# Two-layer graph attention on one core: new timetables for the first two and last three pairs, and another buffer for two output tiles

## The reference, cut to what matters

```
h = maximum(layernorm(x), 0)                      # layer 0
q, k, v = h @ Wq + bq, h @ Wk + bk, h @ Wv + bv   # 8 heads of 64
weights = softmax(q @ k.T / 8 + mask)             # mask: -1e9 where adj == 0
x = x + weights @ v
h = maximum(layernorm(x), 0)                      # layer 1
q, k, v = h @ Wq.T, h @ Wk.T, h @ Wv.T
rel = adj.T * (q @ k.T)
rel = rel / norm(rel, axis=2)
x = x + rel @ v
```

## Time and profile before

| | |
|---|---|
| device time, median of 3 runs | 2420.07 us (2419.92 to 2421.03) |
| profiled execution | 2422.38 us, span 2420.6 us |
| PE busy | 2391.3 us, 99% of the span |
| ACT busy | 1686.1 us, 70% |
| DVE busy | 1454.1 us, 60% |
| POOL busy | 1301.7 us, 54% |

### The profile page before, as it was taken

How to read it: one execution, slowest core, us unless ns; L and a number is a source line. 1 busy time by engine, 2 the same in 40 slices (tenths; PEclk the granted TensorE clock), 3 DMA queues, 4 the chain that set the end, 5 groups by cost and what they waited for, 6 DMA issues and landing times.

```text
span 2420.6 us, 53556 instructions
## 1 busy us (share of the span) xinstructions
PE 2391.3 (99%) x19252; PEld 1299.4 (54%) x19252; DVE 1454.1 (60%) x4435; ACT 1686.1 (70%) x4111; POOL 1301.7 (54%) x1159
## 2 busy tenths in 40 slices
PE   8999999999999999999999999999999999999998
PEld 4455555555555555555555555555555555555554
DVE  5665666655666555665556665556655566655664
ACT  5867777667776677776777766777667777667773
POOL 3655555555555555555555555555555555555561
PEclk9999999999999999999999999999999999999999
DMA  7756676666677566776566765667755667656663
GB/s 206 148 123 125 136 152 140 135 129 130 133 153 140 115 131 133 153 141 128 128 131 144 149 137 121 132 132 153 143 127 127 132 146 149 131 124 135 134 125 70
DMA packets 938361, 328.09 MB, mean 136 GB/s; under 512 B 886000, under 2 KB 886256, under 8 KB 938096
## 3 DMA queue, kind: packets, MB, share of 16 engines
q1 hardware_dynamic: 935312, 319.43, 63.3%
q10 hardware_dynamic: 2784, 5.24, 0.6%
HBM read 72.88 MB, written 33.55 MB: 44 GB/s over the span
## 4 chain that ended last, share of the span: by engine, by line
PE 90%; DMA 2%; ACT 2%; DVE 2%; issue 1%; POOL 1%; DVEq 0%; SPq 0%; ACTq 0%
PE B L728 76%; PE S L804 7%; PE O L728 7%; DMA probs_t<-halves 2%; ACT probs L529 1%; DVE stats L592 0%; ACT h L473 0%; ACT halves L537 0%; DVE masked L665 0%; POOL v L423 0%; DVE rel_halves L699 0%; POOL halves L427 0%; ACT h_halves L480 0%; DVE result L706 0%; DVE v_sum L657 0%
## 5 line engine op out<-in xcount | busy, mean ns | idle before, releaser
L427 POOL TENSOR_TENSOR halves<-probs,halves 128x512 f16<-128x512 f32 x512 | 598.1, 1168 | 561.5 <-ACT halves L537 561.2
L529 ACT ACTIVATE probs<-masked,neg_max 128x256 f32<-128x256 f32 x1024 | 508.3, 498 | 204.4 <-DVE neg_max L665 204.2
L665 DVE CUSTOM_DVE_ANT_0 masked<-S,mask 128x256 f32<-128x256 f32 x1024 | 385.7, 415 | 129.8 <-PE S L804 125.5
L413 POOL TENSOR_TENSOR h_halves<-h,h_halves 128x512 f16<-128x512 f32 x256 | 295.3, 1159 | 155.7 <-ACT h_halves L480 155.7
L728 PE MATMUL B<-wv,h0t 128*128 128x512 f16 x1536 | 354.1, 380 | 3.9 <-DMA h0t<-h_halves 2.5
L728 PE MATMUL B<-h0t,wq 128*128 128x512 f16 x1536 | 352.8, 379 | 0.0
L728 PE MATMUL B<-h0t,wk 128*128 128x512 f16 x1536 | 352.5, 379 | 0.0
L728 PE MATMUL B<-h1t,wm 128*128 128x512 f16 x1488 | 336.5, 379 | 1.3 <-DMA h1t<-h_halves 1.3
L728 PE MATMUL B<-wvt,h1t 128*128 128x512 f16 x1488 | 336.7, 379 | 1.1 <-issue 1.1
L537 ACT ACTIVATE halves<-probs 128x512 f16<-128x512 f32 x512 | 322.6, 630 | 20.3 <-PE O L728 4.2
L728 PEld LDWEIGHTS O<-v,probs_t 128*128 128x128 f16 x6144 | 245.8, 98 | 126.1 <-DMA probs_t<-halves 9.9
(11 more groups left out here) (78 smaller groups left out, 2983.0 us busy)
## 6 DMA issues: line engine op xcount, KB each, us to landing
x_in<-in_x_dram SPq DMA_DIRECT2D x128, 256.0 KB, 3.1
out_dram<-result SPq DMA_DIRECT2D x128, 256.0 KB, 3.4
x_res<-in_x_dram SPq DMA_DIRECT2D x124, 256.0 KB, 3.3
probs_t<-halves SPq DMA_TRANSPOSE x512, 2.8
h0t<-h_halves SPq DMA_TRANSPOSE x132, 3.2
h1t<-h_halves SPq DMA_TRANSPOSE x124, 3.3
rq<-in_L_gnn_Wq_dram ACTq DMA_DIRECT2D x4, 256.0 KB, 4.9
x_res<-in_L_gnn_Wk_dram ACTq DMA_DIRECT2D x4, 256.0 KB, 5.4
```

The costliest lines, as they stand in the source:

```text
L413: nc.gpsimd.tensor_tensor(h_halves[:, n, 1, :], h[:, n % 2, :], h_halves[:, n, 0, :], ALU.subtract).then_inc(h_low[layer], 1)
L427: nc.gpsimd.tensor_tensor(halves[:, n % RING, 1, :], probs[:, n % 2, :, :].rearrange("p t n -> p (t n)"), halves[:, n % RING, 0, :], ALU.s ...
L529: ins = nc.scalar.activation(probs[:, n % 2, i, :], masked[:, n % 2, i, :], ACT.Exp, bias=neg_max[:, n % 2, i:i + 1], scale=-1.0, accum_ou ...
L665: ins = nc.vector.tensor_tensor_reduce(out=masked[:, n % 2, i, :], in0=S[n % 4][:, i, :], in1=mask[:, i, :], scale=SCORE, scalar=BIG, op0= ...
```

## The change

It gives new slots to the steps of pairs 0 and 1 and of pairs 29, 30 and 31, and it writes the third and fourth output tile of pair 31 into `h` (the buffer of the normalized matrices, which has two tiles as `result` has) with a wait on the last low half of `h` in the place of the wait on the stores.

```diff
-    PRODUCT_0 = {("v", 0): 0.5, ("v", 1): 1, ("q", 0): 1.5, ("k", 0): 2.5, ("v", 2): 5, ("v", 3): 7,
-                 ("q", 1): 9, ("k", 1): 10, ("q", 2): 13, ("k", 2): 13.5, ("q", 3): 15, ("k", 3): 22.5}
+    PRODUCT_0 = {("v", 0): 0, ("v", 1): 1, ("q", 0): 2, ("k", 0): 4, ("q", 1): 5.5, ("v", 2): 7.5,
+                 ("k", 1): 8, ("v", 3): 9, ("q", 2): 13.5, ("k", 2): 15.5, ("q", 3): 16.5, ("k", 3): 22.5}
...
+        def out_buffer(n, p):
+
+            return (h if p == PAIRS - 1 and n >= 2 else result)[:, n % 2, :]
+
...
-                    sp.dma_start(ov[p][:, n, :], result[:, n % 2, :]).then_inc(stored[n % 2], 16)
+                    sp.dma_start(ov[p][:, n, :], out_buffer(n, p)).then_inc(stored[n % 2], 16)
...
-                    need(dve, stored[n % 2], 16 * (2 * p + n // 2))
-                    nc.vector.scalar_tensor_tensor(result[:, n % 2, :], B[BANK[kind, n, p]][:, :], 1.0 / WS,
+                    if p == PAIRS - 1 and n >= 2:
+                        dve.wait_ge(h_low[1], TILES * PAIRS)
+                    else:
+                        need(dve, stored[n % 2], 16 * (2 * p + n // 2))
+                    nc.vector.scalar_tensor_tensor(out_buffer(n, p), B[BANK[kind, n, p]][:, :], 1.0 / WS,
```

More of the change, by code:

```diff
@@ L90, in adjacency_attention_two_layers @@
-    PRODUCT_30 = {("rq", 0): 41, ("rq", 1): 42, ("rq", 2): 43, ("rq", 3): 44, ("rel", 0): 45.5,
-                  ("rel", 1): 46, ("rv", 0): 47, ("rv", 1): 48.5, ("rv", 2): 49, ("out", 0): 49.5,
-                  ("rv", 3): 50, ("out", 1): 50.5, ("out", 2): 51, ("out", 3): 51.5}
-    LAYER1_30 = {"ln1_scale": [36.5], "ln1_apply": [37, 37, 38, 38], "ln1_split": [37.5, 37.5, 38, 39],
-                 "squares": [45.5, 46], "rel_scale": [47, 47.5], "rel_split": [47.5, 49]}
-    PRODUCT_31 = {("q", 0): 0.5, ("k", 0): 1, ("v", 0): 2.5, ("q", 1): 4, ("v", 1): 4.5, ("k", 1): 6,
[3 rows of a table removed]
-                  ("out", 0): 41, ("out", 1): 42, ("out", 2): 44, ("out", 3): 46}
@@ new lines, in adjacency_attention_two_layers @@
+    SCORED_0 = [6.5, 11, 19, 26]
+    MASKED_0 = [6.5, 8.5, 12, 13.5, 19, 23.5, 25, 27]
+    MULTIPLIED_0 = [12.5, 12.5, 14, 14, 18.5, 21, 21, 21, 25.5, 27, 28, 28.5, 31, 31.5, 32.5, 34]
+    LAYER0_0 = {"x_res": [10.5, 10.5, 12, 12.5], "residual": [16, 20, 29, 32]}
+    LAYER0_1 = {"x_in": [-27.5, -25, -19.5, -17], "ln0_stats": [-14, -14, -13, -12.5], "ln0_power": [-12.5],
+                "ln0_scale": [-11], "ln0_apply": [-9, -9, -6, -2], "ln0_split": [-7, -7, -5, -2]}
+    PRODUCT_1 = {("v", 0): -2, ("v", 1): 1.5, ("q", 0): 2.5, ("k", 0): 3, ("v", 2): 4.5, ("v", 3): 8.5,
+                 ("q", 1): 9.5, ("k", 1): 10, ("q", 2): 13, ("q", 3): 13.5, ("k", 2): 15, ("k", 3): 23}
@@ new lines, in adjacency_attention_two_layers @@
+    OUT_29 = {("out", 0): 64, ("out", 1): 65, ("out", 2): 66, ("out", 3): 66.5}
+    PRODUCT_30 = {("rq", 0): 41, ("rq", 1): 42, ("rq", 2): 43.5, ("rq", 3): 44, ("rel", 0): 45.5,
+                  ("rel", 1): 46, ("rv", 0): 47.5, ("rv", 1): 48.5, ("rv", 2): 49, ("out", 0): 49,
+                  ("rv", 3): 50, ("out", 1): 50.5, ("out", 2): 51, ("out", 3): 51.5}
+    LAYER1_30 = {"ln1_scale": [36.5], "ln1_apply": [37, 37.5, 38, 38], "ln1_split": [38] * TILES, "squares":
+                 [45.5, 47.5], "rel_scale": [47, 48], "rel_split": [48, 49.5]}
@@ new lines, in adjacency_attention_two_layers @@
+    PRODUCT_31 = {("q", 0): 0, ("v", 0): 0.5, ("k", 0): 1.5, ("q", 1): 3.5, ("v", 1): 5, ("k", 1): 5.5,
[3 rows of a table added]
+                  ("out", 0): 41.5, ("out", 1): 44, ("out", 2): 44.5, ("out", 3): 49.5}
+    SCORED_31 = [3.5, 7.5, 12.5, 15]
+    MASKED_31 = [3.5, 5.5, 8, 9.5, 12.5, 13.5, 15, 16]
+    MULTIPLIED_31 = [7.5, 8, 9.5, 9.5, 12, 12, 12, 12.5, 15, 15, 15, 16.5, 18, 18, 18.5, 19.5]
+    RESIDUAL_31 = {"residual": [10, 14.5, 17.5, 17.5]}
+    LAYER1_31 = {"ln1_stats": [21.5, 21.5, 22.5, 22.5], "ln1_power": [23], "ln1_scale": [23.5], "ln1_apply":
+                 [24, 24.5, 24.5, 25], "ln1_split": [24, 24.5, 25, 25], "squares": [37, 37.5], "rel_scale":
+                 [38.5, 39], "rel_split": [38.5, 40.5]}
```

## The result

| | before | changed |
|---|---|---|
| device time, median of 7 runs each | 2420.74 us (2419.92 to 2421.72) | 2411.16 us (2409.97 to 2413.34) |
| ratio | | 0.9961, 95% interval 0.9952 to 0.997 |
| profiled span | 2420.6 us | 2408.4 us |

A forecast was written before the change was run, and what follows sets the result against it. PE, busy 99% of the span, was taken as the bound, with gaps winnable only at the two ends. Start −5.6 and end −4.3 sum to −9.9 us, from median 2420.07 to 2410.2 us; range 2405.5 to 2416.5.

The forecast's parts named there:

- The start, −5.6: From the second scores to the first `rv`: PE's gaps shrink by 5.6 us in sum, new waits included.
- −3.5 at `v0.1`: First `h0t` of pair 1: its wait falls from 2.52 to 0.45 us and full clock returns 1.44 us.
- The end, −4.3: From `h1t` of pair 30 to the last store: PE saves 4.3 us in sum, new waits included.
- The clock's 1.33 returned: At `out2.30`: with only 0.9 us of wait left, the product runs at full clock and saves 1.33 us.
- +0.5 at `rq0.31`: At `rq0.31`: a new wait of 0.5 us, since PE is now faster than the fourth tile of `h`.
- `out3.29`, +0.1: At `out3.29`: PE waits 0.1 us more.
- 1.26 of `h1t`: Pair 30: `h1t` lands before PE asks for it, so its wait of 1.26 us goes.
- one of my signs of being wrong: Anywhere walked as free: a wait of over 1 us there would show the prediction wrong.
- the port rival: Layer-norm scales of pairs 1, 30, 31: each meets one more blocking POOL operation, +3.0 us, 2413.2 us; chance 0.12.
- The side engines set the start: Start: the chain to `h0t` moves only with ACT's fifth `exp`, gaining 2.8 us, total 2413.0 us; chance 0.15.
- The change does nothing: Start's gaps only move, as later pairs keep the old tables: 2420 us, give or take 2; chance 0.1.
- slower through the store of `out0.29`: Pair 29: a later-issued store holds DVE at `out2.29`, and PE waits; 12.5 us late gives 2421 us; chance 0.06.

The follow-up runs named there:

- e1: The new tables of pairs 0 and 1 alone, put into the kernel before: 2415.57 us, ratio 0.9981.
- e4: The kernel before with only the loads of `x_res` of pair 0 issued earlier: 2420.61 us, ratio 1.0.
- e11: The kernel before with only `residual0.31` moved early, from slot 15 to 10: 2423.16 us, one run.
- e8: The kernel before with only the new slots of the products and scores of pair 0: 2418.53 us, ratio 0.9997.
- e2: The new tables of pairs 29, 30 and 31 alone in the kernel before, without the other output buffer: 2418.30 us, ratio 0.9992.
- e3: The kernel before with only the third and fourth output tile of pair 31 written into `h`: 2420.51 us, ratio 1.0.
- e9: The changed kernel with only `residual0.31` moved late, from slot 10 to 13: 2412.14 us, ratio 0.9963 against the kernel before.
- e5: The kernel before with the new residual and layer-norm order of pair 31 and a few late steps of pairs 30 and 31: 2417.76 us, ratio 0.9992.

## Why the prediction was right, and where not

**The start, −5.6: right in sum.** Measured −6.07 in the profile, −4.6 by e1's ratio. The 6.07 is all in PE's gaps: from the first `v0.0` to the first `rv` they are 7.38 us before, with 1.44 more for the slow product, and 2.75 us after. The waits at the second scores, at `k1.1` and at the first `rv` went as walked; `k1.1` even lost the 0.95 that I had left it. New waits came at other sizes: `h0t` 1.01 (I said 0.45), `q0.1` 0.42 (1.0), and two for `probs_t` that I had not walked to, 0.58 and 0.74 us. I had written that no `pv` is asked for within 3 us of its transpose; that is wrong, and the 0.53 that I took off for it is not a gain. `q0.1` came 4.61 us nearer to the first `v0.0`, 0.35 of it because one `pv` now stands behind it; my terms up to it add to 4.45. The 73.9 that I named for its start is not what these terms give (79.49 − 4.45 = 75.04, or 74.69 with the `pv`), and it stood at 75.43.

**The reason given for the largest term was wrong.** Of the −3.5 at `v0.1`, 1.44 us was "the clock's, returned". e4 (full clock, `q0.1` at 55.76) and e11 (full clock, 55.81, behind waits of 0.54 and 0.91 us for `probs_t`) show that the low clock cost nothing here; PE would have waited for ACT instead. The gain came since ACT's `exp` and halves moved with PE: the fourth high half of `h` stands 3.39 us earlier in the changed kernel, where I had written 4.05. e8 shows it from the other side: with the products alone ACT moves 0.97 us and the first `rv` 0.8 us.

**The end, −4.3: too large; measured −2.65 in the profile, −2 by e2's ratio without the buffer.** Two terms failed.

- *"The clock's 1.33 returned" at `out2.30`.* I added it beside the wait, and put +0.5 at `rq0.31` for PE now being faster than the fourth tile. e3 shows that this tile was late by 1.42 us already as soon as the clock doesn't fall. What counts is how much earlier the tile itself comes: PE waits for it at 29.37 us behind `rel0.30` in e3 and at 26.11 in the changed kernel. PE's own −0.8, −2.04 and −1.33 are not all to be had beside it: I had −3.7 from `rel0.30` to `rq0.31`, and 29.25 to 26.11 is −3.14.
- *`out3.29`, +0.1 where the wait grew by 0.87.* That ate most of the 1.26 of `h1t`, which did go. e9 and e11 show the cause: a second POOL operation beside the scale of pair 30, where my walk had counted one. From `rv0.29` to `rel0.30` I had −0.36; with that operation out of the way e9 has −0.33, in the changed kernel it is +0.75. (A wait of 0.34 us for `k_st` at a `scores` some 55 us ahead of `rel0.30` was in neither walk nor rival; e9 has it too.) A wait of over 1 us at a place walked as nearly free was one of my signs of being wrong, and here it stood. This was the port rival, to which I gave 0.12. It asked for one more such meeting in each of pairs 1, 30 and 31; it came in pair 30 alone (in pair 31 all these operations take 0.16 us, in pair 1 two take 1.56 together where one took 1.13), and cost 1.08 us and not 3. The Trainium skill, "SBUF — State Buffer", section "SBUF: two separate sides", has DVE held for the whole of POOL's operation where both want the shared port pair and POOL's began first; by that rule the trace agrees, 1.08 us beside a POOL operation of 1.15, and where nothing stands beside it 0.16.

The other terms: `pv10.31` +0.9, measured 0.61 + 0.20 there; 0.45 at `rel0.30` stays, measured 0.45; `rv1` −0.8, its wait is gone; 0.9 left at `out2.30`, measured 0.87; last store −0.2, measured −0.24 in e3. The walk's "31 periods" between 166 and 2240 us are 28, at 74.1 us each (2149.22 for 29); no term hangs on it.

**The sum** was −9.9 from 2420.07, and the median fell by 9.6 (7.3 to 11.6 by the ratio's interval). By the markers the parts I had walked gave 8.7 and not 9.9: the start 0.5 us more than I had, the end 1.65 less. So the agreement of −9.9 with −9.6 is in part chance: errors of both signs, and the scatter of the medians. The 0.9 us between 8.7 and 9.6 is within what the medians leave open.

**The other rivals.** "The side engines set the start" was right on who sets it (e4) and wrong on the sum, since the change moves them too. "The change does nothing" and "slower through the store of `out0.29`" did not come: that store delayed nothing that PE waited for, and `out3.29` waited for `k_st`.

## What to carry to other kernels

A gap on the bounding engine is worth only what the next gap behind it leaves: before a low clock or a wait is booked as gain, look whether the next thing it needs would be there earlier. Where a stretch is set by two queues in step, changing the order of one gives little: here the products alone gave an eighth (0.8 of 6 us). When a POOL operation on 128x512 is moved, look at which small DVE operations it comes to stand beside: here 1.27 us in a free place of POOL's cost PE 1.08.

## What the runs showed of the hardware that I had not expected

**The clock did not fall each time behind the same gap.** At `v0.1` the wait was 2.52 us in before and the product took 4.19; with 2.58 in e3 4.14, with 2.61 in e5 4.27, with 2.63 in e2 5.28, but with 2.65 in e11 2.75. This is e11's row:

```profile
69.30 2.75 PE L728 MATMUL B<-wv,h0t 128*128 128x512 f16 x12 [2.65 <-DMA h0t<-h_halves]
```

and this e2's:

```profile
69.46 5.28 PE L728 MATMUL B<-wv,h0t 128*128 128x512 f16 x12 [2.63 <-DMA h0t<-h_halves]
```

At `out2.30`, behind the same wait of 2.9, it took 4.08 (before), 4.07 (e4), 4.44 (e1), 4.43 (e11), 5.28 (e8) and 2.75 us (e3). Only the two longest, of 5.28 us, reached past the next wait: e2's `q0.1` is 1.24 us later than that of before, and e8 takes 30.68 us from `rel0.30` to `rq0.31` in the place of 29.25.

**The pairs that nobody changed vary by 4 us.** From `rv0.0` to `rv0.29` the 13 profiled executions take 2145.19 to 2149.22 us, and the two ends of that are the changed kernel and before. PE's idle time in front of the `pv` in this stretch, 170 to 2235 us, nearly all of it for `probs_t`, is part of it: this row of the changed kernel, grouped by line, stands against the earlier trace rows.

```profile
L735 PE MATMUL O<-v,probs_t 128*128 128x64 f16 x5352 | 228.8, 193 | 0.9 <-DMA probs_t<-halves 0.9
```

In the others it is 0.8 to 2.7, in before 3.1, and it is not sorted by the edits: 0.8 in e2 with the old start tables, 1.8 in e1 with the new. It accounts for 2.2 of the 4.0 us; I did not find the rest. The runs with the new start tables average 2146.3 us in this stretch and the others 2147.6, with a spread of about 1 us in each, so whether the new start still gives something there stays open.
